# Copies ahead of exponentials, attention's first steps before the loop's turn, and scans and outer products spread singly over the steps

## The chip, the core and the metric

The kernel runs on one core of a Trainium2 chip. The core has engines that work side by side and meet only at semaphores: TensorE (PE, matrix products and transposes, results in PSUM), VectorE (DVE), ScalarE (ACT, exponentials and copies), GpSimd (POOL) and SyncE (SP, which issues most DMAs). Each engine works through its own instructions in program order. The metric is the device time of one launch in microseconds, the median of several runs; a profiled execution has a time of its own, and all rows below come from it.

## What is computed

Two layers run over 8 sequences of 512 tokens with 256 features. The change touches the second layer alone, and in it two parts that the kernel runs side by side for each sequence: a recurrence with a state of 16 by 16 for each of 16 heads, and causal softmax attention with 16 heads.

```python
# recurrence (the "scan"), for each head
def step(st, inp):
    rt, wt, kt, vt = inp
    kv = jnp.einsum('bhi,bhj->bhij', kt, vt)            # outer product
    y = jnp.einsum('bhi,bhij->bhj', rt, st + uh[None, :, :, None] * kv)
    return (wt[..., None] * st + kv, y)
...
# attention
q = jnp.concatenate([q_nope, _rope(q_rope)], axis=-1)
k = jnp.concatenate([kv, _rope(k_rope)], axis=-1)
att = jnp.einsum('bhqd,bhkd->bhqk', q, k) / jnp.sqrt(jnp.float32(D))
att = jnp.where(mask, att, jnp.float32(-jnp.inf))
att = jax.nn.softmax(att, axis=-1)
y = jnp.einsum('bhqk,bhkd->bhqd', att, v)
...
# what is around them
x = x + s * g        # s: recurrence, g: silu of (attention + experts)
```

## The kernel before

`phase_c` does the second layer, one sequence of 512 tokens after the other. For each engine it has two functions: `before_attention(b)` (projections, mixing, and the rotation of the queries) and `attention(b)` (attention, the recurrence, then gating and nine experts). Every engine calls `before_attention(0)`, then loops over `attention(b)` and `before_attention(b + 1)` for b = 0 to 6, and then calls `attention(7)`. So the turn of the loop, a branch on each engine, lies between `before_attention` and `attention`. The experts' part of `attention` is left as it is.

**Queries.** In `before_attention` PE makes eight products q0 to q7 (two heads each). DVE rotates them (`rotate`, L1700 and L1701: one product with the cosines, one shuffle), POOL finishes each (L1884, L1886). DVE's rotation n waits until POOL has finished rotation n-2, since there are two shuffle buffers. Between q5 and q6 DVE also does `outer(0)`, `scan(0)` and `outer(1)` of the recurrence.

**The 32 steps of attention.** A step i is a pair of heads and one tile of 128 queries; i % 4 sets how many keys it sees: 128, 256, 384 or 512. For one step:

- PE `scores(i)` (L1155, with the mask L1158): two score tiles in banks 0 and 1 for even i, 2 and 3 for odd i. It waits until `exp(i-2)` has read these banks.
- DVE `highest(i)` (L1631): the row maxima, read from PSUM.
- ACT `exp(i)` (L1454): two exponentials, into four probability tiles; it waits until those of step i-2 are transposed.
- PE `turn_probs(i)` (L1172): transposes the probabilities into banks 5 and 6. It waits for `exp(i)` and until the copies of step i-1 have freed the banks, and stands in PE's order right after `scores(i+2)`.
- ACT `keep(i)` (L1463): two copies of the transposed tiles to SBUF. They stand in ACT's order in front of `exp(i+3)`.

After every eight steps PE does `weigh_values(g)` (L1202, probabilities times values, 64 short products), which needs the copies of the group's last step; ACT copies its result (L1472), PE spreads the inverse row sums (`spread_inverse`, L1191), DVE scales (L1665). `weigh_values(0)` stands on PE behind `turn_probs(8)`, thus between `scores(10)` and `scores(11)`, and likewise 8 and 16 steps later.

**The recurrence beside it.** 32 units n, 24 of them during attention. One unit is DVE `outer(n)` (L1644, reads a copy of a value row that SP fetched, writes `kv`), DVE `scan(n)` (L1651, the recurrence over 512 tokens) and POOL `product(n)` (L1897, state times receptance); PE sums four products at a time (`reduce_state`, L1182). In three of four steps (`UNIT_STEP`, i % 4 not 3) DVE does `scan(n)` and `outer(n+1)` right after `highest(i)`; in the fourth it does `highest(i)` alone. `outer` and `scan` read two operands from SBUF, `highest` and the rotations read PSUM.

## Time and profile before

| | us |
|---|---|
| median of three runs | 2815.42 |
| lowest and highest run | 2812.85, 2822.94 |
| profiled execution | 2818.96 |
| its span in the trace | 2817.1 |
| PE busy in the span | 2302.9 (82%) |
| DVE busy | 1749.2 (62%) |
| ACT busy | 930.0 (33%) |
| POOL busy | 931.9 (33%) |

The span is what the trace covers; the 1.9 us beside it are outside the engines' work. A sequence of the second layer takes some 258 us, of which the 32 steps of attention take 96. The first exponential of the eight sequences starts at 805.00, 1066.66, 1324.93, 1581.95, 1840.59, 2099.63, 2359.03 and 2616.34 us.

### The profile page before, as it was taken

The numbers are of one execution on the slowest core, as the hardware profiler recorded it, in microseconds if no ns is written. First come the engines' busy times: TensorE is split into PE (matmuls) and PEld (weight loads), VectorE is DVE, ScalarE is ACT, GpSimd is POOL, SyncE is SP. The second block draws the span as 40 slices with busy tenths as digits, with TensorE's granted clock in tenths as the row PEclk, the third lists the DMA queues.
The fourth block names the chain that finished last, engine by engine and source line by source line (L and its number), as shares of the span: only waits on it lengthen the run. The fifth ranks groups of instructions, "written<-read, shape, count | busy, mean of one in ns | idle before, by whom it ended". The sixth has DMA issues, their size and how long they took to land.

```text
span 2817.1 us, 35706 instructions
## 1 busy us (share of the span) xinstructions
PE 2302.9 (82%) x9632; PEld 1248.1 (44%) x9633; DVE 1749.2 (62%) x2951; ACT 930.0 (33%) x2466; POOL 931.9 (33%) x722
## 2 busy tenths in 40 slices
PE   7887599996877886798889778967988897788777
PEld 3443366664434533443444345334434443453344
DVE  5777344443276657675756677576757566765766
ACT  2333133231135224412532351254125323522441
POOL 2113200001164245415432542453154325423531
PEclk9998799998788998898989899988989898999889
DMA  4342411013022112201210221122012102211210
GB/s 138 112 143 62 148 30 30 26 30 98 8 57 54 34 31 61 68 1 50 63 48 15 58 54 34 31 61 68 0 49 62 49 7 62 57 34 30 61 46 8
DMA packets 139997, 146.16 MB, mean 52 GB/s; under 512 B 47025, under 2 KB 99889, under 8 KB 139825
## 3 DMA queue, kind: packets, MB, share of 16 engines
q1 hardware_dynamic: 132530, 131.49, 17.2%
q0 software_dynamic: 3072, 8.41, 0.9%
q10 hardware_dynamic: 4224, 4.19, 0.4%
q8 instruction: 81, 1.33, 0.2%
q14 instruction: 90, 0.74, 0.1%
HBM read 116.48 MB, written 27.43 MB: 51 GB/s over the span
## 4 chain that ended last, share of the span: by engine, by line
PE 27%; issue 24%; DVE 10%; POOL 9%; ACT 4%; DVEq 0%; DMA 0%; POOLq 0%; ACTq 0%
PE bank L1284 13%; PE bank L1172 4%; DVE arena L1631 3%; POOL arena L1879 3%; PE bank L1155 3%; ACT arena L1454 3%; POOL arena L1884 2%; DVE arena L1651 2%; PE bank L1202 2%; DVE arena L1644 2%; PE bank L1182 2%; POOL arena L1886 2%; ACT arena L1463 1%; PE bank L1109 1%; PE bank L1191 1%
## 5 line engine op out<-in xcount | busy, mean ns | idle before, releaser
L1897 POOL TENSOR_TENSOR arena<-arena 128x512 f32<-128x512 f32 x256 | 385.1, 1505 | 619.5 <-DVE arena L1651 603.7
L1109 PE MATMUL bank<-arena 128*128 128x512 f32 (+2 forms) x896 | 444.5, 644 | 40.9 <-ACT arena L1415 22.2
L1284 PE MATMUL bank<-arena 128*128 128x512 f32 (+2 forms) x1312 | 445.6, 495 | 6.3 <-ACT arena L1419 6.3
L1454 ACT ACTIVATE arena<-bank,arena 128x128 f32<-128x128 f32 (+3 forms) x512 | 266.0, 524 | 468.3 <-DVE arena L1631 410.4
L1172 PE MATMUL bank<-arena 128*128 128x128 f32 x1280 | 234.8, 318 | 187.2 <-ACT arena L1463 185.9
L1651 DVE TENSOR_TENSOR_SCAN arena<-arena 128x512 f32<-128x512 f32 x256 | 346.4, 1353 | 8.1 <-issue 7.8
L1284 PEld LDWEIGHTS bank<-arena 128*128 128x128 f32 x1312 | 255.8, 209 | 190.9 <-issue 154.2
L1631 DVE TENSOR_REDUCE arena<-bank 128x2 f32<-128x256 f32 (+3 forms) x256 | 207.5, 821 | 190.4 <-PE bank L1158 177.3
L1109 PEld LDWEIGHTS bank<-arena 128*128 128x128 f32 (+2 forms) x896 | 166.3, 195 | 299.9 <-issue 235.4
L1155 PE MATMUL bank<-arena 64*128 64x128 f32 (+3 forms) x1024 | 235.1, 540 | 63.6 <-ACT arena L1454 63.6
L1172 PEld LDWEIGHTS bank<-arena 128*128 128x128 f32 x1280 | 168.9, 163 | 224.6 <-ACT arena L1454 190.3
L269 PE MATMUL bank<-arena 128*128 128x512 f32 x384 | 189.6, 647 | 34.3 <-DVE arena L423 18.0
L1644 DVE TENSOR_TENSOR arena<-arena 128x512 f32<-128x512 f32 x256 | 210.7, 823 | 0.0
L1463 ACT ACTIVATE arena<-bank 128x128 f32<-128x128 f32 (+3 forms) x512 | 197.1, 440 | 12.8 <-PE bank L1172 12.2
L1879 POOL TENSOR_TENSOR arena<-arena 128x512 f32<-128x512 f32 x80 | 103.2, 1309 | 220.2 <-DVE arena L1676 220.2
L1155 PEld LDWEIGHTS bank<-arena 64*128 64x128 f32 x1024 | 86.9, 208 | 145.1 <-ACT arena L1454 81.0
L702 PE MATMUL bank<-arena 128*128 x624 | 145.6, 385 | 1.3 <-ACT arena L736 1.3
L682 PE MATMUL bank<-arena 128*128 x312 | 143.5, 603 | 1.2 <-DVE arena L777 1.2
L1884 POOL TENSOR_TENSOR arena<-arena 128x512 f32<-128x512 f32 x72 | 103.6, 1438 | 116.4 <-DVE arena L1701 116.2
L1676 DVE SCALAR_TENSOR_TENSOR arena<-bank,arena 128x512 f32<-128x512 f32 x80 | 58.5, 741 | 128.8 <-PE bank L1109 126.1
L269 PEld LDWEIGHTS bank<-arena 128*128 128x128 f32 x384 | 75.9, 204 | 131.1 <-issue 90.4
L1415 ACT ACTIVATE arena<-bank 128x512 f32<-128x512 f32 (+1 forms) x96 | 55.6, 595 | 230.1 <-PE bank L1109 230.0
(201 smaller groups left out, 2955.8 us busy)
## 6 DMA issues: line engine op xcount, KB each, us to landing
arena<-values SPq DMA_DIRECT2D x256, 256.0 KB, 3.5
arena<-in_L_attn_h SPq DMA_DIRECT2D x16, 512.0 KB, 3.6
arena<-in_W1T SPq DMA_DIRECT2D x8, 1024.0 KB, 5.7
arena<-in_W2T SPq DMA_DIRECT2D x8, 1024.0 KB, 8.6
sorted_rows<-arena SPq DMA_DIRECT2D x42, 128.5 KB, 9.3
arena<-sorted_rows SPq DMA_DIRECT2D x40, 128.5 KB, 2.1
gate_rows<-arena SPq DMA_DIRECT2D x39, 128.0 KB, 1.7
s_rows<-arena ACTq DMA_DIRECT2D x8, 512.0 KB, 3.0
```

Of the source, the lines that this page charges most:

```text
L269: last = nc.tensor.matmul(bank[s + q][:, :], gru_w[layer][:, k, q * D + m * P:q * D + (m + 1) * P], src[:, k, :], start=(k == 0), stop=(k ...
L1109: last = nc.tensor.matmul(dst[rows, :], w, x, start=(n == 0), stop=(n == len(pairs) - 1))
L1155: nc.tensor.matmul(bank[2 * (i % LAG) + half][:, 0:n], qT[rows, p, qt * P:(qt + 1) * P], ckvT[rows, 0:n], start=True, stop=False)
L1172: last = nc.tensor.transpose(bank[5 + half][:, kt * P:(kt + 1) * P], probs[s % PROBS][:, kt * P:(kt + 1) * P], ident)
L1284: last = nc.tensor.matmul(dst[o], w, x, start=first, stop=last_one)
L1454: nc.scalar.activation(probs[s % PROBS][:, 0:n], bank[2 * (i % LAG) + half][:, 0:n], ACT.Exp, bias=neg_max[:, s:s + 1], accum_out=row_sum[ ...
L1463: nc.scalar.activation(turned[h % HGROUP][:, 0:qt + 1, qt * P:(qt + 1) * P], bank[5 + half][:, 0:(qt + 1) * P].rearrange("p (k c) -> p k c ...
L1631: nc.vector.tensor_reduce(neg_max[:, 2 * i:2 * i + 2], psum[:, at:at + 1024].rearrange("p (h k) -> p h k", h=2)[:, :, 0:n], X, ALU.max, ne ...
L1644: nc.vector.tensor_tensor(kv[n % 2], copies[n % COPIES], proj["k"][:, n // HD, :], ALU.mult).then_inc(kv_done, 1)
L1651: nc.vector.tensor_tensor_scan(state[n % STATES][:, 1:T + 1], proj["w"][:, m, :], kv[n % 2], VEC["init"][:, m * HD + j:m * HD + j + 1], AL ...
L1879: nc.gpsimd.tensor_tensor(mix[n % 2][:, m, :], mix[n % 2][:, m, :], xnT[:, m, :], ALU.add).then_inc(mixed, 1)
L1897: nc.gpsimd.tensor_tensor(prods[n % PRODS], state[n % STATES][:, 0:T], proj["r"][:, m, :], ALU.mult).then_inc(prod_done, 1)
```

## The change

Four edits, all in `phase_c`:

1. ACT does the copies `keep(i-2)` in front of `exp(i)`; before, it did `keep(i-3)` there.
2. PE issues `scores(0)` behind q5 and `scores(1)` behind q6, DVE does `highest(0)` behind the rotation of q5 and `highest(1)` behind that of q6, all of this before the turn of the loop. `outer(0)` moves to behind the rotation of q3; `scan(0)` and `outer(1)` move behind the turn, into step 1. DVE's wait on `w_step` goes to the end of `before_attention`.
3. `PARTS` spreads the outer products and scans: two of them in even steps and in steps 1 and 3, one in the other odd steps, in the order scan, outer, scan, outer. It is 24 scans and 24 outer products either way.
4. `weigh_values(g)` for g = 0, 1, 2 moves on PE from behind `turn_probs` to in front of `scores` of the same step (10, 18, 26). The last one stays behind the first part of the output product.

```diff
-UNIT_STEP = [i for i in range(PSTEPS) if i % NT != NT - 1]
-EARLY = len(UNIT_STEP)
+EARLY = 24
+def parts_by_step():
+    parts = [("scan", 0)]
+    for n in range(1, EARLY):
+        parts += [("outer", n), ("scan", n)]
+    parts.append(("outer", EARLY))
+    steps, at = [[]], 0
+    for i in range(1, PSTEPS):
+        n = 2 if i % 2 == 0 or i in (1, 3) else 1
+        steps.append(parts[at:at + n])
+        at += n
+    return steps
+PARTS = parts_by_step()
+UNIT_STEP = [i for i in range(PSTEPS) for name, n in PARTS[i] if name == "scan"]
...
@@ PE, before_attention
                         product(b, name, [(q_w[:, k, i * P:(i + 1) * P], xbT[:, k, :]) for k in range(KD)])
+                        if name in ("q5", "q6"):
+                            scores(b, int(name[1]) - 5)
@@ PE, attention
-                for i in range(PSTEPS + LAG + 3):
+                for i in range(LAG, PSTEPS + LAG + 3):
+                    if GSTEPS + 2 <= i < PSTEPS and (i - GSTEPS - 2) % GSTEPS == 0:
+                        weigh_values(b, (i - GSTEPS - 2) // GSTEPS)
                     if i < PSTEPS:
                         scores(b, i)
-                    if LAG <= i < PSTEPS + LAG:
+                    if i < PSTEPS + LAG:
                         turn_probs(b, i - LAG)
...
                         wo(1, 0, range(GROUPS - 1))
-                    if i >= GSTEPS + 2 and (i - GSTEPS - 2) % GSTEPS == 0:
-                        weigh_values(b, (i - GSTEPS - 2) // GSTEPS)
+                        weigh_values(b, GROUPS - 1)
@@ ACT, attention
-                    if LAG < i <= PSTEPS + LAG:
-                        keep(2 * (i - LAG - 1))
-                        keep(2 * (i - LAG - 1) + 1)
+                    if LAG <= i < PSTEPS + LAG:
+                        keep(2 * (i - LAG))
+                        keep(2 * (i - LAG) + 1)
                     if i < PSTEPS:
                         exp(2 * i)
                         exp(2 * i + 1)
@@ DVE, before_attention
-                        if name == "q5":
+                        if name == "q3":
                             outer(b, 0)
-                            v.wait_ge(w_step, 2 * b + 2)
-                            scan(b, 0)
-                            outer(b, 1)
+                        elif name in ("q5", "q6"):
+                            highest(b, m - 5)
+                v.wait_ge(w_step, 2 * b + 2)
@@ DVE, attention
-                    if i < PSTEPS:
+                    if LAG <= i < PSTEPS:
                         highest(b, i)
...
-                    if i in UNIT_STEP and i > 0:
-                        unit(b, UNIT_STEP.index(i))
+                    for name, n in PARTS[i] if i < PSTEPS else []:
+                        (scan if name == "scan" else outer)(b, n)
@@ POOL, attention
-                    if i in UNIT_STEP:
-                        product(UNIT_STEP.index(i))
+                    for n in [n for n in range(EARLY) if UNIT_STEP[n] == i]:
+                        product(n)
```

DVE around the turn of the loop, from the rotation of q4 on, before (L1700 and L1701 are a rotation, L1644 is `outer`, L1651 `scan`, L1631 `highest`; ISA and register rows are waits and branches):

```order
L1700 TENSOR_TENSOR arena<-bank,arena 128x512
L1701 STREAM_SHUFFLE arena<-bank 128x512
L1644 TENSOR_TENSOR arena<-arena 128x512
L1651 SCALAR_TENSOR_TENSOR arena<-arena 128x512
L1644 TENSOR_TENSOR arena<-arena 128x512
L1700 TENSOR_TENSOR arena<-bank,arena 128x512
L1701 STREAM_SHUFFLE arena<-bank 128x512
L1700 TENSOR_TENSOR arena<-bank,arena 128x512
L1701 STREAM_SHUFFLE arena<-bank 128x512
L1843 UNCONDITIONAL_BRANCH
L1843 ISA
L1631 TENSOR_REDUCE arena<-bank 128x2
```

and in the changed kernel, from the rotation of q5 on (lines are 21 higher: L1652 is `highest`, L1672 `scan`, L1665 `outer`, L1721 and L1722 a rotation):

```order
L1721 TENSOR_TENSOR arena<-bank,arena 128x512
L1722 STREAM_SHUFFLE arena<-bank 128x512
L1652 TENSOR_REDUCE arena<-bank 128x2
L1721 TENSOR_TENSOR arena<-bank,arena 128x512
L1722 STREAM_SHUFFLE arena<-bank 128x512
L1652 TENSOR_REDUCE arena<-bank 128x2
L1721 TENSOR_TENSOR arena<-bank,arena 128x512
L1722 STREAM_SHUFFLE arena<-bank 128x512
L1864 UNCONDITIONAL_BRANCH
L1864 ISA
L1672 SCALAR_TENSOR_TENSOR arena<-arena 128x512
```

Between the rotations of q5 and q6 three operations of the recurrence are gone and the first two maxima stand among the rotations instead; the first operation behind the branch is now a scan.

ACT's first steps of a sequence, before (L1454 are the exponentials, L1463 the copies; 128x2x128 is a copy of 256 columns):

```order
L1454 ACTIVATE arena<-bank,arena 128x128 x2
L1454 ACTIVATE arena<-bank,arena 128x256 x2
L1454 ACTIVATE arena<-bank,arena 128x384 x2
L1463 ACTIVATE arena<-bank 128x128 x2
L1454 ACTIVATE arena<-bank,arena 128x512 x2
L1463 ACTIVATE arena<-bank 128x2x128 x2
L1454 ACTIVATE arena<-bank,arena 128x128 x2
```

and in the changed kernel (L1475 exponentials, L1484 copies):

```order
L1475 ACTIVATE arena<-bank,arena 128x128 x2
L1475 ACTIVATE arena<-bank,arena 128x256 x2
L1484 ACTIVATE arena<-bank 128x128 x2
L1475 ACTIVATE arena<-bank,arena 128x384 x2
L1484 ACTIVATE arena<-bank 128x2x128 x2
L1475 ACTIVATE arena<-bank,arena 128x512 x2
L1484 ACTIVATE arena<-bank 128x3x128 x2
```

Each pair of copies now stands one pair of exponentials earlier.

PE at step 10, before (L1155 and L1158 are scores, L1172 transposes, L1202 `weigh_values`):

```order
L1155 MATMUL bank<-arena 128x384 x2
L1158 MATMUL bank<-arena 128x128 x2
L1168 REGISTER_ALU
L1172 MATMUL bank<-arena 128x128 x2
L1202 MATMUL bank<-arena 32x512 x4
```

and in the changed kernel (L1173 and L1176 scores, L1190 transposes, L1220 `weigh_values`):

```order
L1190 MATMUL bank<-arena 128x128 x8
L1220 MATMUL bank<-arena 32x512 x4
L1220 MATMUL bank<-arena 32x384 x4
L1220 MATMUL bank<-arena 32x256 x4
L1220 MATMUL bank<-arena 32x128 x4
L1170 REGISTER_ALU
L1173 MATMUL bank<-arena 128x384 x2
```

`weigh_values` now stands between the transposes of step 7 and the scores of step 10.

## Rows read from the trace of the kernel before

**Rows 1.** Busy us by stage: PE, weight loads, DVE, ACT, POOL; PEclk, DMA.

```profile
1066.60:1163.00 96.40, 72.16 (x486) 38.21 (x486) 73.64 (x88) 57.06 (x191) 44.05 (x30) 0.89 0.26 64
2099.17:2195.09 95.92, 73.48 (x486) 39.39 (x486) 72.16 (x86) 55.40 (x185) 43.98 (x29) 0.88 0.24 61
2108.00:2116.00 8.00, 5.90 (x26) 3.86 (x24) 4.84 (x7) 5.27 (x18) 2.30 (x3) 0.57 0.29 67
```

**Rows 2.** Waits from 2099 to 2197 us: who waited for whom, total, times, longest.

```profile
DVE arena L1631 <- PE bank L1158: 22.4, 15, 4.1
PE bank L1172 <- ACT arena L1463: 20.3, 24, 2.2
DVE arena L1651 <- issue: 1.3, 1, 1.3
```

**Rows 3.** Timeline (start, us, engine, line), exponentials of step 7 to those of step 9.

```profile
2120.44 0.69 ACT L1454 ACTIVATE arena<-bank,arena 128x512 f32<-128x512 f32 x1 [1.34 <-DVE arena L1631]
...
2121.72 1.27 DVE L1651 TENSOR_TENSOR_SCAN arena<-arena 128x512 f32<-128x512 f32 x1
2121.78 0.66 ACT L1463 ACTIVATE arena<-bank 128x256 f32<-128x256 f32 x2
2122.30 0.85 PE L1172 MATMUL bank<-arena 128*128 128x128 f32 x6 [0.96 <-ACT arena L1463]
...
2122.91 0.67 DVE L1644 TENSOR_TENSOR arena<-arena 128x512 f32<-128x512 f32 x1
2123.08 0.70 PE L1155 MATMUL bank<-arena 64*128 64x256 f32 x4
...
2124.04 0.69 DVE L1631 TENSOR_REDUCE arena<-bank 128x2 f32<-128x512 f32 x1 [0.46 <-PE bank L1158]
...
2124.86 0.47 ACT L1454 ACTIVATE arena<-bank,arena 128x256 f32<-128x256 f32 x1 [0.42 <-PE bank L1172]
```

**Rows 4.** Timeline around the turn of the loop.

```profile
2088.83 1.27 POOL L1884 TENSOR_TENSOR arena<-arena 128x512 f32<-128x512 f32 x1
...
2090.15 0.67 DVE L1644 TENSOR_TENSOR arena<-arena 128x512 f32<-128x512 f32 x1
...
2090.86 2.17 DVE L1651 TENSOR_TENSOR_SCAN arena<-arena 128x512 f32<-128x512 f32 x1
...
2096.41 0.74 DVE L1701 STREAM_SHUFFLE arena<-bank 128x512 f32<-128x512 f32 x1
...
2099.17 1.02 DVE L1631 TENSOR_REDUCE arena<-bank 128x2 f32<-128x256 f32 x2 [2.02 <-issue]
...
2101.52 2.23 DVE L1651 TENSOR_TENSOR_SCAN arena<-arena 128x512 f32<-128x512 f32 x1 [1.32 <-issue]
```

**Rows 5.** Timeline, the copies of step 7 and `weigh_values(0)` behind them.

```profile
2124.19 1.06 PE L1172 MATMUL bank<-arena 128*128 128x128 f32 x8 [0.19 <-ACT arena L1463]
...
2125.77 1.09 ACT L1463 ACTIVATE arena<-bank 128x512 f32<-128x512 f32 x2
...
2127.24 2.37 PE L1202 MATMUL bank<-arena 128*32 128x512 f32 x32
```

**Rows 6.** Chain that ended last (start, us, what): PE work between transposes and scores.

```profile
2134.97 0.89 PE bank L1191 x8
2135.86 1.00 PE bank L1182 x8
```

**Rows 7.** Timeline at the end of the steps.

```profile
2193.88 1.21 DVE L1631 TENSOR_REDUCE arena<-bank 128x2 f32<-128x1024 f32 x1
...
2196.37 1.63 POOL L1897 TENSOR_TENSOR arena<-arena 128x512 f32<-128x512 f32 x1 [1.45 <-DVE arena L1651]
...
2196.55 0.66 ACT L1463 ACTIVATE arena<-bank 128x256 f32<-128x256 f32 x2
...
2196.95 2.13 DVE L1651 TENSOR_TENSOR_SCAN arena<-arena 128x512 f32<-128x512 f32 x1
...
2198.27 1.94 PE L1172 MATMUL bank<-arena 128*128 128x128 f32 x8 [0.23 <-ACT arena L1463]
```

1 line of the change is left out of this document (added).

## The prediction, written before the changed kernel ran

> **What bounds the kernel now.** I read four views in this order: busy time by stage, the waits of the stage, the timeline of two steps, and the timeline around the turn of the loop. In the stage of the 32 steps, from the first `highest` at 2099.17 to the end of the last at 2195.09, no engine is full: of 95.92 us PE is busy 73.5, DVE 72.2, ACT 55.4, POOL 44.0, and another sequence shows the same [rows 1]. So the stage is bound by waiting in rings. DVE's idle time is 95.92 - 72.16 = 23.8 us; 22.4 of it is `highest` waiting for the scores, in 15 places, and 1.3 is a stall in which it waits for nothing shown [rows 2].
>
> Why the scores are late is seen in two steps [rows 3]. The exponentials of step 7 start at 2120.44. Behind them ACT does the copies of step 5 (2121.78), only then may PE transpose step 6 (2122.30, after 0.96 us of waiting for the copies), behind that stand the scores of step 9 (2123.08), then `highest(9)` (2124.04, 0.46 idle) and the exponentials of step 9 (2124.86). That ring takes 4.4 us for two steps, although the scores of step 9 need only the exponentials of step 7. PE waits 20.3 us in all for copies [rows 2].
>
> **Copies ahead of exponentials.** After the change the copies of step 5 stand in front of the exponentials of step 7, where ACT waits for `highest(7)` anyway. When the exponentials of step 7 end (2121.78), step 6 is no longer held up by a copy behind them. The ring that remains is exponentials, scores, then the later of two branches, exponentials. From the end of scores that see 256 keys, the longer branch is half the transposes of 512 columns (0.5), a hand-off (0.15) and both copies (1.09) [rows 5], then two exponentials of 256 (0.94), a hand-off and scores of 512 (about 1.3): 4.1 us. From there `highest` (1.21) [rows 7], exponentials of 512 (1.34, from 2120.44 to 2121.78), hand-offs and scores of 256 (0.85) [rows 3]: 3.7 us. Together 7.8 us for four steps, against 96/8 = 12.0 now. DVE's own work is 72.2/8 = 9.0 us for four steps. So DVE becomes the bound, with 1.2 us of slack for the ring.
>
> **Even spreading.** DVE's work is the same, but the port to SBUF that it shares with POOL now costs it something. In the trace a scan that started at 2196.95 inside a product of POOL's (2196.37 to 2198.00) took 2.13 us instead of 1.27, so that it ended 1.08 after the product did [rows 3, 7]. Before, `outer` follows its scan at once and is ahead of the product (1.27, then 0.67) [rows 3]. Singly spread, a product starts 0.15 us after its scan and runs 1.3 to 1.6 us, while DVE does only `highest` (0.4 to 1.2) before its next two-operand operation: that is caught for 0.2 to 0.5 us in three of four steps, 1.1 us per four steps. Where DVE has a wait or `scale_values` in between, it costs nothing; I take half, 0.5 us times 7 groups of four steps, 3.5 us (ends 0 and 7.7).
>
> The Trainium skill states this as a rule, in SBUF — State Buffer, section "Who interferes with whom": an exclusive lock of the shared port pair for a whole instruction when VectorE has two SBUF inputs and GpSimd reads SBUF. By that rule the change is charged in full, the 7.7 us end. The scan at 2196.95, which finished only after the product, agrees with it.
>
> **`weigh_values` in front of the scores.** This adds a wait, at steps 10, 18 and 26. From the end of `scores(9)` it takes the transposes' first half and the copies of step 7 (1.9, as above), a hand-off (0.1), 2.3 us of `weigh_values` (2127.24 to 2129.6) [rows 5], the scores of 384 keys (1.1) and a hand-off (0.1): 5.5 us until `highest(10)` may start. DVE has in this time, with 0.4 us of lag, `highest(9)` (0.61), a reciprocal (0.2) and a scan (1.2 to 1.5): 2.6 us. Behind the waiting `highest(10)` stand the outer product and scan of the step. DVE waits 2.8 us, three times: 8.4 (ends 5 and 10, by the lag). Other waits for scores: 0.6.
>
> **The beginning.** Before, DVE did outer, scan, outer from 2090.15 on, the scan at 2.17 instead of 1.27 since POOL was busy, and the rotation of q7 ended at 2097.15 [rows 4]. Now only the two `highest` (1.0 together) stand among the rotations, and POOL sets the pace: its first half for q4 starts at 2088.83, it takes 2 x 1.27 for each, so q5 is done at 2093.9. `outer(0)` behind q3 now runs beside POOL and puts it back by about 0.5: 2094.4. DVE's rotation of q7, 1.4 to 1.5, waits for that and ends at 2095.9, 1.25 us earlier. The turn's stall of 2.0 us [rows 4] stays; it comes in front of `scan(0)` now. The exponentials of steps 0 and 1 are done by then, but this brings nothing more: DVE is the bound here.
>
> **DVE's account of the stage.** From the end of the turn's stall to the end of the last `highest`: 72.2, less `highest` of steps 0 and 1 (1.0), plus `scan(0)` (1.2; `outer(1)` comes in, `outer(24)` goes out), plus the second stall (1.3), the port (3.5), and the waits (8.4 + 0.6): 86.2 us instead of 95.9. That is 9.7, with the beginning 1.2: 10.9 us.
>
> **The end.** After the exponentials of step 31, ACT still did the copies of step 29 (2196.55), PE transposed step 30, ACT copied it, and the transposes of step 31 started at 2198.27 [rows 7]. Now the copies of step 29 are done before. One copy and a hand-off plus half the transposes of step 30 go, about 1.0 us, and what follows (the rest of the sequence) is untouched and shifts as a whole. SP's fetches and POOL's products have time to spare: with four buffers of each, an operation of unit n waits for one of unit n-4, some 12 us back, and POOL is busy 44 of 96 us [rows 1].
>
> **Sum.** 10.9 + 1.0 = 11.9 us per sequence, times 8 = 95 us. Against the profiled 2818.96 this is 2724; it lies 3.5 us above the median 2815.42, so that the median should go to **2720** (-3.4%).
>
> **Rivals.**
>
> *PE's other work takes the place of the copies.* `reduce_state` (1.00, six times) and `spread_inverse` (0.89, three times) [rows 6] also stand between transposes and scores. The ring has only some 1.2 us of slack per four steps, and at steps 12 and 28 two of them come together. If all are exposed, 6.0 + 2.7 = 8.7 us of the gain go: 3.2 us per sequence, 26 us, 2790. For it: 0.89 and 1.00 stand on the chain that ended last in the trace of before. Against: that chain ran through them because the copies made PE late.
>
> *The port is paid in full.* 7.7 instead of 3.5, and `outer(0)` twice as dear: 7.2 us per sequence, 58 us, 2758. For it: the scan at 2196.95. Against: waits absorb part of it.
>
> *The change does little.* The exponentials wait for `turn_probs` of step i-2 as before, and now for the copies too. If hand-offs of the longer chain through both cost 0.3 us more in each of 32 steps (9.6), 2 us per sequence are left: 2800, within 0.5% or just beyond. Against: ACT is busy 55 of 96 us and has room [rows 1].
>
> *Slower: PE stays at its lower clock.* The granted clock is 0.88 in the stage and was 0.57 from 2108 to 2116 us [rows 1], after PE had waited for the first exponentials; 0.5 is the 1.2 GHz level, 1.0 is 2.4 GHz. PE's 73.5 busy us are 73.5 x 0.88 = 64.7 at full clock. If the new pattern of short pieces kept it at the lower level, PE would need 129 us: 33 more per sequence, 264 in all, 3080. It decides from a granted clock of 64.7/96 = 0.67 downward; at 0.60 it would be 12 us per sequence slower, 2910. Against: PE will wait less in total, not more.
>
> *More than forecast.* The port costs nothing (3.5 us), and the waits of `weigh_values` are at their lower end (3.4): some 16 us per sequence with a little for half-clock stretches that DVE now hides, 126 us, 2690.
>
> **Chances.** Forecast as worked out (9.5 to 14 us per sequence, 2704 to 2740) 0.48; port in full 0.20; PE's other work 0.13; little change 0.06; slower 0.05; more 0.08. The range goes from 2692 to 2788: it takes in the port in full and almost all of PE's other work. A measurement of this kernel can tell about 0.5% (14 us) from no change. Faster by more than that 0.88 (a third of "little change" and three quarters of PE's other work are in it), within it 0.07, slower 0.05.
>
> **What the profile after would show.** Right: DVE's wait for the scores falls from 22.4 to about 9 us per stage and stands at steps 10, 18 and 26, about 2.8 each; PE's wait for copies all but vanishes from the transposes; the stage takes 86 us; the rotation of q7 ends 1.2 us earlier against the rotation of q5. Port: means of L1672 and L1665 of some 1.4 and 0.8 us, with long ones inside products. PE's other work: `highest` waits at steps 8, 13, 18, 24 and 29 too. The prediction is wrong if the first steps after the turn stall for longer than 3.3 us, or if DVE waits for scores in most steps.

## The result, and the profile of the changed kernel

The changed kernel takes **2690.22 us** (median of four runs, 2685.88 to 2691.32) against 2814.14 (2808.63 to 2822.94) for the kernel before, measured side by side: the ratio is 0.9554, with a 95% interval of 0.9527 to 0.9581. That is 4.5% faster, where 3.4% and 2720 us were forecast. It lies 1.8 us below the low end of the range, 2692. The profiled execution took 2691.32 us, its span is 2689.5.

The eight first exponentials start at 787.67, 1032.59, 1274.48, 1517.99, 1762.48, 2006.04, 2250.72 and 2494.24 us. From the second to the seventh that is 243.6 us per sequence; before, it was (2359.03 - 1066.66)/5 = 258.5. So a sequence became 14.9 us shorter, not 11.9.

The stage first. This is the view of busy time by stretch that answers to [rows 1]: length, then busy us of PE, weight loads, DVE, ACT and POOL, then PEclk, DMA share and GB/s. The first row is the stage of the 32 steps in a typical sequence, from the first scan behind the turn to the end of the last `highest`; the other two are pieces of it around step 18.

```profile
1768.90:1852.00 83.10, 65.19 (x482) 35.66 (x480) 73.47 (x85) 53.14 (x178) 40.16 (x29) 0.92 0.27 74
1804.00:1810.00 6.00, 3.29 (x24) 1.94 (x26) 5.96 (x8) 3.70 (x13) 2.16 (x2) 1.00 0.19 48
1810.00:1813.60 3.60, 3.60 (x22) 1.67 (x26) 3.23 (x5) 3.35 (x12) 3.09 (x2) 0.65 0.52 146
```

DVE is now busy 73.5 of 83.1 us, 88%, where it was 75% of 95.9 [rows 1]. It is the bound, with 83.1 - 73.5 = 9.6 us of idle time. The waits of the stage (who waited for whom, total, times, longest; 1773.9 to 1852 us) say what that time is:

```profile
DVE arena L1652 <- PE bank L1176: 9.4, 4, 4.3
PE bank L1190 <- ACT arena L1484: 1.2, 1, 1.2
```

`highest` (L1652) waits 9.4 us for the scores (L1176), in four places, instead of 22.4 in 15 [rows 2]. The transposes (L1190) wait once for a copy (L1484), instead of 24 times for 20.3 us [rows 2]. The ring through the copies is gone. Three of the four waits in the timeline (start, us, engine, line, and in brackets the idle time before); the fourth is 0.32 us:

```profile
1794.71 0.96 DVE L1652 TENSOR_REDUCE arena<-bank 128x2 f32<-128x768 f32 x1 [2.69 <-PE bank L1176]
...
1817.52 0.96 DVE L1652 TENSOR_REDUCE arena<-bank 128x2 f32<-128x768 f32 x1 [4.30 <-PE bank L1176]
...
1838.37 0.96 DVE L1652 TENSOR_REDUCE arena<-bank 128x2 f32<-128x768 f32 x1 [2.05 <-PE bank L1176]
```

They are steps 10, 18 and 26, the steps in which `weigh_values` stands in front of the scores. The timeline of step 10 shows it, and answers to [rows 3, 5]:

```profile
1790.03 1.09 ACT L1484 ACTIVATE arena<-bank 128x512 f32<-128x512 f32 x2
...
1790.67 1.34 DVE L1672 TENSOR_TENSOR_SCAN arena<-arena 128x512 f32<-128x512 f32 x1
1790.90 1.97 POOL L1925 TENSOR_TENSOR arena<-arena 128x512 f32<-128x512 f32 x1
...
1791.24 2.36 PE L1220 MATMUL bank<-arena 128*32 128x512 f32 x32 [0.82 <-ACT arena L1484]
...
1793.54 0.92 PE L1173 MATMUL bank<-arena 64*128 64x384 f32 x4
```

The copies of step 7 end at 1791.12, `weigh_values(0)` (L1220) takes 2.36 us, and only then come the scores of step 10 (L1173, 1793.54), and `highest(10)` may start at 1794.71. DVE had finished its scan at 1792.01 and waited 2.7 us. (L1925 is POOL's widening of the inverse row sums; it matters below.)

Around the turn of the loop, the answer to [rows 4]:

```profile
1756.64 1.64 DVE L1665 TENSOR_TENSOR arena<-arena 128x512 f32<-128x512 f32 x1
...
1766.57 0.73 DVE L1722 STREAM_SHUFFLE arena<-bank 128x512 f32<-128x512 f32 x1
...
1768.92 1.89 DVE L1672 TENSOR_TENSOR_SCAN arena<-arena 128x512 f32<-128x512 f32 x1 [1.63 <-issue]
...
1770.73 1.68 DVE L1665 TENSOR_TENSOR arena<-arena 128x512 f32<-128x512 f32 x1
```

The rotation of q7 ends at 1767.30. Behind the branch DVE stalls for 1.63 us and then runs on without the second stall of 1.32 that [rows 4] shows.

At the end of the steps, the answer to [rows 7]:

```profile
1850.76 1.20 DVE L1652 TENSOR_REDUCE arena<-bank 128x2 f32<-128x1024 f32 x1
...
1853.97 1.94 PE L1190 MATMUL bank<-arena 128*128 128x128 f32 x8 [2.51 <-ACT arena L1484]
```

The last transposes start 1853.97 - 1851.96 = 2.0 us after the last `highest`; before it was 2198.27 - 2195.09 = 3.2 [rows 7].

### The profile page after: what moved, and what is told of

Same layout as the page of the kernel before. It is cut to its first block, busy times and chain, and to the rows that moved or that the text cites. A ratio compares the mean times of both kernels' runs of the same rounds, so it can differ in the third digit from the quotient of the medians.

```text
span 2689.5 us, 36104 instructions
## 1 busy us (share of the span) xinstructions
PE 2252.5 (84%) x9632; PEld 1219.3 (45%) x9633; DVE 1748.6 (65%) x2951; ACT 924.5 (34%) x2466; POOL 886.6 (33%) x722
## 3 DMA queue, kind: packets, MB, share of 16 engines
q8 instruction: 81, 1.33, 0.2%
## 4 chain that ended last, share of the span: by engine, by line
issue 26%; PE 24%; DVE 11%; POOL 10%; ACT 2%; DVEq 0%; DMA 0%; POOLq 0%; ACTq 0%
PE bank L1304 14%; DVE arena L1672 3%; DVE arena L1665 3%; POOL arena L1900 3%; POOL arena L1905 3%; DVE arena L1652 3%; PE bank L1220 2%; PE bank L1173 2%; POOL arena L1907 2%; PE bank L1127 1%; ACT arena L1475 1%; PE bank L1200 1%; PE bank L1190 1%; ACT arena L1484 1%; PE bank L1133 1%
## 5 line engine op out<-in xcount | busy, mean ns | idle before, releaser
L1918 POOL TENSOR_TENSOR arena<-arena 128x512 f32<-128x512 f32 x256 | 343.2, 1341 | 587.0 <-DVE arena L1672 574.8
L1672 DVE TENSOR_TENSOR_SCAN arena<-arena 128x512 f32<-128x512 f32 x256 | 356.4, 1392 | 12.2 <-issue 10.0
L1475 ACT ACTIVATE arena<-bank,arena 128x128 f32<-128x128 f32 (+3 forms) x512 | 266.3, 530 | 247.5 <-DVE arena L1652 247.5
L1304 PEld LDWEIGHTS bank<-arena 128*128 128x128 f32 x1312 | 256.4, 210 | 193.6 <-issue 157.1
L1173 PE MATMUL bank<-arena 64*128 64x128 f32 (+3 forms) x1024 | 223.7, 516 | 129.5 <-ACT arena L1475 119.8
L1652 DVE TENSOR_REDUCE arena<-bank 128x2 f32<-128x256 f32 (+3 forms) x256 | 207.5, 811 | 79.9 <-PE bank L1176 79.9
L1484 ACT ACTIVATE arena<-bank 128x128 f32<-128x128 f32 (+3 forms) x512 | 199.6, 442 | 121.0 <-PE bank L1190 120.9
L1190 PE MATMUL bank<-arena 128*128 128x128 f32 x1280 | 208.6, 300 | 36.9 <-ACT arena L1484 29.7
L1665 DVE TENSOR_TENSOR arena<-arena 128x512 f32<-128x512 f32 x256 | 204.2, 798 | 0.0
L1173 PEld LDWEIGHTS bank<-arena 64*128 64x128 f32 x1024 | 83.5, 199 | 220.4 <-ACT arena L1475 166.4
L1190 PEld LDWEIGHTS bank<-arena 128*128 128x128 f32 x1280 | 155.5, 155 | 45.0 <-ACT arena L1475 33.1
L1900 POOL TENSOR_TENSOR arena<-arena 128x512 f32<-128x512 f32 x80 | 103.1, 1309 | 214.2 <-DVE arena L1697 214.2
L1905 POOL TENSOR_TENSOR arena<-arena 128x512 f32<-128x512 f32 x72 | 99.9, 1388 | 113.2 <-DVE arena L1722 112.9
L269 PEld LDWEIGHTS bank<-arena 128*128 128x128 f32 x384 | 74.9, 201 | 127.5 <-issue 89.1
```

Of the source, the lines that this page charges most:

```text
L269: last = nc.tensor.matmul(bank[s + q][:, :], gru_w[layer][:, k, q * D + m * P:q * D + (m + 1) * P], src[:, k, :], start=(k == 0), stop=(k ...
L1173: nc.tensor.matmul(bank[2 * (i % LAG) + half][:, 0:n], qT[rows, p, qt * P:(qt + 1) * P], ckvT[rows, 0:n], start=True, stop=False)
L1190: last = nc.tensor.transpose(bank[5 + half][:, kt * P:(kt + 1) * P], probs[s % PROBS][:, kt * P:(kt + 1) * P], ident)
L1304: last = nc.tensor.matmul(dst[o], w, x, start=first, stop=last_one)
L1475: nc.scalar.activation(probs[s % PROBS][:, 0:n], bank[2 * (i % LAG) + half][:, 0:n], ACT.Exp, bias=neg_max[:, s:s + 1], accum_out=row_sum[ ...
L1484: nc.scalar.activation(turned[h % HGROUP][:, 0:qt + 1, qt * P:(qt + 1) * P], bank[5 + half][:, 0:(qt + 1) * P].rearrange("p (k c) -> p k c ...
```

## The account of one sequence

A mark that both kernels share is DVE's scaling of the transposed `xb` in `before_attention`: it stands behind the sequence's mixing and right ahead of the rotations. From it to the end of the last `highest` a typical sequence took 125.4 us before and takes 110.9 now, 14.5 less.

| part (us; stalls and ends: what is gained) | forecast | measured |
|---|---|---|
| rotation of q7 ends earlier | 1.25 | 1.28 |
| first stall behind the turn (2.0 before) shorter | 0 | 0.4 |
| second stall (1.3 before) gone | 0 | 1.3 |
| waits for the scores that remain (length) | 9.0 | 9.4 to 9.6 |
| stage from first scan to last `highest` (length) | 86.2 | 83.0 |
| mark to last `highest`, gain | 10.9 | 14.5 |
| end of the steps | 1.0 | -0.4 to 0.9 |
| whole sequence | 11.9 | 14.9 |

In the stage I had 77.2 us of DVE work with the port and the second stall in it; it is 73.5, 3.7 less: 1.3 of stall and 2.4 of port.

## Experiments

Every kernel ran beside the kernel before on one chip; the groups of experiments ran on different chips, whose medians for the kernel before lie between 2813.7 and 2816.1 us. The ratio to the kernel before is given with each. "Mark to last `highest`" is the length of the table above, for the typical sequences of the kernel's profile.

### How much the first phases scatter

Up to the first sequence of the second layer the two kernels run the same code, yet the first rotation of the changed kernel's profile came 9.8 us earlier (770.1 against 779.9). Is that the change or chance? The two kernels ran again, unchanged.

> The kernel before once more, unchanged, for a second profile. The profile after started the second layer's rotations 9.8 us earlier than the profile before (770.1 against 779.9 us), in phases that the change does not touch. Theory A (scatter from one execution to the next): this profile lies at 770 to 780 us for the first rotation. Theory B (the change moves code and so changes the first phases): it lies at 779 to 781 again.

> The changed kernel once more for a second profile: the first rotation lay at 770.1 us in the first one. Theory (scatter of the first phases): anywhere from 770 to 782 us, with the stage of 32 steps unchanged (110.9 us from the scaling of xb to the end of the last highest). Rival (the change moves code and so speeds the first phases): 769 to 771 again.

The kernel before took 2812.5 us, with its first rotation at 774.9 and 125.5 us from mark to last `highest`; the changed one took 2695.5, with the first rotation at 774.6 and 110.9. So the same program moves by 5 us, and over all fourteen profiles the first rotation lies between 770 and 782 us. It is chance: the length of a typical sequence repeats to 0.1 us, while the phases ahead of it scatter over 12 us, 0.4% of the whole. The 1.8 us by which the range was missed are less than that, and this second run lies inside it; the distance to the forecast of 2720 is not chance.

### The parts alone

**Copies ahead of exponentials alone**: the kernel before with this one edit.

```diff
-                    if LAG < i <= PSTEPS + LAG:
-                        keep(2 * (i - LAG - 1))
-                        keep(2 * (i - LAG - 1) + 1)
+                    if LAG <= i < PSTEPS + LAG:
+                        keep(2 * (i - LAG))
+                        keep(2 * (i - LAG) + 1)
```

> The kernel before with only the copies of step i-2 ahead of the exponentials of step i; weigh_values, first steps and recurrence stay as they were. Theory (the ring through the copies bound the stage): most of the gain, 8 to 10 of the 14.7 us per sequence, 2735 to 2750 us; waits of highest for scores fall from 22.4 to some 12 us. Rival (the gain lies at the turn of the loop): 2800 to 2815.

It took 2691.71 us (2688.81 to 2697.68), ratio 0.956 [0.9528, 0.9593]: the whole gain of the change, with one of its four edits. Mark to last `highest` is 110.4 us in the middle, 109.0 to 113.5 in the loop, although this kernel still has both stalls and the late rotation of q7. The waits of a stage (L1631 is `highest`, L1158 the scores, as in the kernel before) and the place where `weigh_values` (L1202) stands here, behind the scores of step 10 (L1155, 1796.98) and the transposes of step 8:

```profile
DVE arena L1631 <- PE bank L1158: 7.9, 9, 1.6
```

```profile
1796.98 0.92 PE L1155 MATMUL bank<-arena 64*128 64x384 f32 x4
...
1798.28 2.36 PE L1202 MATMUL bank<-arena 128*32 128x512 f32 x32
...
1799.49 0.95 DVE L1631 TENSOR_REDUCE arena<-bank 128x2 f32<-128x768 f32 x1
1800.36 1.27 DVE L1651 TENSOR_TENSOR_SCAN arena<-arena 128x512 f32<-128x512 f32 x1
```

`highest(10)` starts without a wait while PE is at `weigh_values`: that work lies wholly beside DVE's. My expectation was 43 to 58 us too slow, since I had credited the other edits with the rest.

**Even spreading alone**: `PARTS` in the kernel before, with `outer(0)`, `scan(0)` and `outer(1)` left ahead of the turn.

```diff
-UNIT_STEP = [i for i in range(PSTEPS) if i % NT != NT - 1]
+        n = 2 if i % 2 == 0 else 1
+        steps.append(parts[at:at + n])
...
-                    if i in UNIT_STEP and i > 0:
-                        unit(b, UNIT_STEP.index(i))
+                    for name, n in PARTS[i] if i < PSTEPS else []:
+                        (scan if name == "scan" else outer)(b, n)
```

> The kernel before with only the scans and outer products spread singly over the steps; copies behind the exponentials, as before. Theory: the ring through the copies is still there, so DVE's order moves nothing but its waits: 2800 to 2815. Rival (DVE's uneven order is what made scores late): 2760 to 2785.

2818.32 us over ten runs, ratio 1.0004 [0.9987, 1.0022]: no change. Its waits are those of [rows 2] (L1648 `highest`, L1175 scores, L1189 transposes, L1480 copies):

```profile
DVE arena L1648 <- PE bank L1175: 22.8, 13, 4.5
PE bank L1189 <- ACT arena L1480: 18.8, 24, 2.2
```

While DVE waits 22 us for scores, it doesn't matter in which steps its work stands.

**The first steps alone**: the second edit of the change in the kernel before, with scan and outer product in pairs in steps 1, 2, 3 and then three of four.

```diff
+    at = [1, 2, 3] + [i for i in range(4, PSTEPS) if i % NT != NT - 1]
+    for n, i in enumerate(at):
+        steps[i] = [("scan", n), ("outer", n + 1)]
...
-                        if name == "q5":
+                        if name == "q3":
                             outer(b, 0)
-                            v.wait_ge(w_step, 2 * b + 2)
-                            scan(b, 0)
-                            outer(b, 1)
+                        elif name in ("q5", "q6"):
+                            highest(b, m - 5)
```

> The kernel before with only the first steps moved ahead of the turn of the loop, scans and outer products in pairs as before. Theory: 1.3 us of the rotations, 0.4 and 1.3 us of the two stalls behind the turn, 3.0 us per sequence, 24 us: 2785 to 2795. Rival (the ring makes up for a late start): under 8 us, 2807 or more.

2793.69 us (2782.99 to 2798.36), ratio 0.9915 [0.9884, 0.9945]: 22 us, as expected. Mark to last `highest` is 122.1, 3.3 less than before. The row behind the turn (L1665 is the scan) shows one stall where there were two, and the waits show that the ring through the copies stands as it was (L1645 `highest`, L1184 transposes, L1477 copies):

```profile
1822.26 1.62 DVE L1665 TENSOR_TENSOR_SCAN arena<-arena 128x512 f32<-128x512 f32 x1 [1.88 <-issue]
```

```profile
PE bank L1184 <- ACT arena L1477: 23.5, 24, 5.8
DVE arena L1645 <- PE bank L1170: 20.1, 15, 4.1
```

So the sum of the parts, -124 for the copies, -22 for the first steps and 0 for spreading, is 22 us more than the change as a whole brought. If the parts simply added up, the fourth edit would cost that much. They don't quite, as the runs below show: the copies and the first steps together bring 131 us, not 146.

### What `weigh_values` in front of the scores costs

First on top of the copies alone, then taken out of the changed kernel in two ways.

```diff
                 for i in range(PSTEPS + LAG + 3):
+                    if GSTEPS + 2 <= i < PSTEPS and (i - GSTEPS - 2) % GSTEPS == 0:
+                        weigh_values(b, (i - GSTEPS - 2) // GSTEPS)
                     if i < PSTEPS:
```

> copies_only with weigh_values (0) to (2) in front of the scores of their step, and nothing else of the change. Theory (its place costs 5 to 6 us per sequence whatever the order of DVE): 2730 to 2742. Rival (it costs only when DVE is the bound everywhere, and copies_only has waits of its own, 7.9 us): 2700 to 2715.

2709.15 us (2706.08 to 2711.46), ratio 0.9616 [0.9598, 0.9634]: 17 us slower than the copies alone, in the range of the rival and not of the theory. The intervals are just apart. Mark to last `highest` goes to 113 to 114 us, the waits for scores from 7.9 to some 11.

The changed kernel with `weigh_values` 0 to 2 back behind the transposes, where they stood before:

```diff
-                    if GSTEPS + 2 <= i < PSTEPS and (i - GSTEPS - 2) % GSTEPS == 0:
-                        weigh_values(b, (i - GSTEPS - 2) // GSTEPS)
...
-                        weigh_values(b, GROUPS - 1)
+                    if i >= GSTEPS + 2 and (i - GSTEPS - 2) % GSTEPS == 0:
+                        weigh_values(b, (i - GSTEPS - 2) // GSTEPS)
```

> The changed kernel with weigh_values(0) to (2) behind turn_probs of their step, as in the kernel before. In the profile after, highest waits 9.4 us per sequence in the steps of weigh_values (2.7, 4.3, 2.05); in copies_only weigh_values ran behind scores and transposes while DVE had work. Theory (the position of weigh_values costs): these waits fall to under 4 us, 5 to 6 us per sequence, 2640 to 2655. Rival (PE must do it anyway, and the copies that wait for it then hold up the exponentials): 2685 to 2700.

2658.79 us (2651.40 to 2685.04), ratio 0.9475 [0.9416, 0.9535]: 31 us faster than the changed kernel, or 22 by the ratios. One of the four runs took 2685, so that the interval touches that of the changed kernel (from 0.9527); what decides is the profile, and the next run. Mark to last `highest` is, behind the first sequence, 104.6 in four and 106.1 to 107.7 in three, instead of 110.9 to 113.7. The row of the waits (here L1651 is `highest`):

```profile
DVE arena L1651 <- PE bank L1176: 2.2, 5, 0.7
```

9.4 us of waits became 2.2, and 110.9 became 104.6. The edit that was part of the change cost 6.3 us in a typical sequence, and it sits in the three waits that the prediction had priced at 8.4. I had counted them as the price of the new order without asking what the old place would cost once the copies were out of the way.

And between the scores and the transposes of the same step:

> The changed kernel with weigh_values between scores and turn_probs of steps 10, 18 and 26. highest of the step no longer waits for it, but the transposes, the copies behind them and the exponentials of the step do. Theory: DVE has 2.9 us of work per step pair before it needs the exponentials of step 10, so 3 to 5 us per sequence are won, 2650 to 2665. Rival (exponentials become late instead): within 8 us of 2690.

2655.05 us (2651.39 to 2666.69), ratio 0.943 [0.9403, 0.9456], 105.0 to 107.9 us per sequence: the same as behind the transposes, and here the interval is clear of the changed kernel's. What matters is that the scores stand ahead of `weigh_values`; whether the transposes do too can't be seen.

### What even spreading is worth when DVE is the bound

Spreading alone brought nothing since DVE waited. It might in the other kernels. First, pairs in the changed kernel, `weigh_values` still in front:

```diff
-    parts = [("scan", 0)]
-    for n in range(1, EARLY):
-        parts += [("outer", n), ("scan", n)]
...
+    at = [1, 2, 3] + [i for i in range(4, PSTEPS) if i % NT != NT - 1]
+    for n, i in enumerate(at):
+        steps[i] = [("scan", n), ("outer", n + 1)]
```

> The changed kernel with scans and outer products in pairs in three of four steps; weigh_values stays in front. In the profile after a scan took 1.40 us on average, in copies_only 1.35, since products of POOL run when the scan comes. Theory (the single spreading costs by the shared port, about 1.2 us per sequence): 2676 to 2684. Rival (it evens DVE's waits out and is worth something): 2695 to 2710.

2697.79 us (2687.53 to 2701.65), ratio 0.9574 [0.9542, 0.9605]. Neither theory's sign shows: mark to last `highest` is 111.0 in typical sequences, as in the changed kernel (110.9), and so are the waits (L1646 is `highest`):

```profile
DVE arena L1646 <- PE bank L1170: 9.4, 9, 3.4
```

The 7.6 us in the median are within what the first phases scatter; in this profile they ended 12 us later (first rotation at 782.4). In the stage the scan takes 1.33 us in the mean instead of 1.40 and `outer` 0.84 instead of 0.79; the two differences cancel.

What the two orders pay at the port is told under the port term below.

Then pairs with `weigh_values` behind, which is the copies and the first steps together:

> Copies ahead and the first steps ahead of the turn, but scans and outer products in pairs in three of four steps and weigh_values behind turn_probs, as in the kernel before. The two good parts together. Theory (weigh_values in front and the single spreading cost what the first steps gain): copies alone 2692 less 3.2 us per sequence, 2660 to 2672. Rival (the copies alone already use up what can be had, DVE's slack takes the start): 2685 to 2695.

2683.15 us (2675.97 to 2686.29), ratio 0.9538 [0.9512, 0.9564], longer than expected. The profile shows two lengths within one kernel, behind the first sequence: 106.05 us in three and 110.25 in four. This is the same stretch of a short sequence (first two rows) and of a long one (last two), the columns as above:

```profile
1794.25:1802.25 8.00, 4.91 (x38) 2.98 (x39) 7.61 (x11) 5.68 (x22) 4.09 (x3) 1.00 0.26 67
1802.25:1810.25 8.00, 7.86 (x73) 3.54 (x72) 7.42 (x10) 4.95 (x17) 5.32 (x4) 1.00 0.29 90
...
2032.70:2040.70 8.00, 4.92 (x32) 2.68 (x33) 7.24 (x10) 5.68 (x22) 4.09 (x3) 0.85 0.25 67
2040.70:2048.70 8.00, 8.00 (x60) 3.74 (x60) 6.09 (x7) 2.42 (x9) 4.39 (x4) 0.72 0.29 68
```

The granted clock stays at 1.00 in the one, and in the other it falls to 0.85 and 0.72 in the mean of a stretch: it is at its 1.2 GHz level (0.50) from 2038.29 to 2045.12. The pieces on PE's path show it, `reduce_state` (L1194) first in the short sequence, then in the long one:

```profile
1802.66 1.07 PE L1194 MATMUL bank<-arena 128*32 128x512 f32 x8
...
2042.56 1.94 PE L1194 MATMUL bank<-arena 128*32 128x512 f32 x8
```

DVE's busy time falls from 7.42 to 6.09 in that stretch, since it waits for scores. 4.2 us are lost in such a sequence. In the 8 us right ahead of the fall PE had been busy 6.00 us, and 5.99 in the same stretch of the short sequence. Why the clock fell in one and not in the other, no run here tells.

Against these, single spreading with `weigh_values` behind has 104.6 us (short) and 106.1 to 107.7 (long), and its long ones lie beside a fall too: 1.5 us better in the short ones, 2.5 to 4.1 in the long ones. Over the whole kernel it is 2683 to 2659, by intervals that overlap a little (0.9512 to 0.9564, 0.9416 to 0.9535), while the profiles show it in both kinds of sequence. So even spreading is worth something once nothing else holds DVE up. Whether it also softens a fall of the clock is not shown, since the falls were smaller there too: 0.92 in the mean of a long sequence's stage, against 0.89 with pairs (0.94 in the short ones of both). In the changed kernel the waits in front of `highest` in steps 10, 18 and 26 hide it.

### The port between DVE and POOL

I had charged the single order with 3.5 us of contention. How much of it is POOL's product? Here each product covers only 128 of its 512 columns; the other 384 are left out. The rest is the kernel with `weigh_values` behind.

```diff
-nc.gpsimd.tensor_tensor(prods[n % PRODS], state[n % STATES][:, 0:T], proj["r"][:, m, :], ALU.mult)
+nc.gpsimd.tensor_tensor(prods[n % PRODS][:, 0:P], state[n % STATES][:, 0:P], proj["r"][:, m, 0:P], ALU.mult)
```

> weigh_behind with POOL's products cut from 512 to 128 columns; the other 384 columns of each product are left out, so that the recurrence's output lacks them. It measures the price of the shared port under the products alone. In weigh_behind a scan takes 1.39 and an outer product 0.82 us on average against 1.27 and 0.67 undisturbed, 6.5 us per sequence, of which the rotations and three widenings of the inverse row sums make about 4. Theory (products that run under the single parts cost little, since a product alone takes 1.09 us): 0.5 to 2.5 us per sequence, 2638 to 2655. Rival (port paid as the prediction charged it, 3.5 us): under 2632.

2632.32 us (2629.75 to 2634.55), ratio 0.9346 [0.9328, 0.9364]: 26 us less. But the stage did not get shorter: mark to last `highest` is 104.1 to 107.2, against 104.6 to 107.7. The groups of all scans (busy us, mean ns), first with whole products, then with short ones:

```profile
L1671 DVE TENSOR_TENSOR_SCAN arena<-arena 128x512 f32<-128x512 f32 x256 | 355.0, 1387 | 12.3 <-issue 10.0
```

```profile
L1671 DVE TENSOR_TENSOR_SCAN arena<-arena 128x512 f32<-128x512 f32 x256 | 329.6, 1287 | 13.0 <-issue 10.7
```

The products cost a scan 0.1 us in the mean. Summed over a typical stage, the scans get 2.5 us shorter and the outer products 1.7, so that whole products cost DVE 4.2 us in this kernel, more than the theory's 0.5 to 2.5. But what DVE saves it waits for scores instead: its wait rises from 2.2 to 5.7 us. Of the 21 us between the two profiled executions (2653.91 and 2632.99), 6.6 are an earlier end of the first phases; the rest lies outside the steps of attention, and its place is open. The 2632.32 lies at the edge of the rival's range: DVE's operations got shorter by what the rival said and more, but attention did not.

What a product costs the next operation is seen in two places of the kernel with `weigh_values` behind (L1917 product, L1664 `outer`, L1671 scan, L1651 `highest`):

```profile
1821.53 1.20 DVE L1651 TENSOR_REDUCE arena<-bank 128x2 f32<-128x1024 f32 x1
1821.69 1.09 POOL L1917 TENSOR_TENSOR arena<-arena 128x512 f32<-128x512 f32 x1 [2.20 <-DVE arena L1671]
...
1822.64 0.69 DVE L1664 TENSOR_TENSOR arena<-arena 128x512 f32<-128x512 f32 x1
...
1824.57 0.67 DVE L1664 TENSOR_TENSOR arena<-arena 128x512 f32<-128x512 f32 x1
1824.73 1.63 POOL L1917 TENSOR_TENSOR arena<-arena 128x512 f32<-128x512 f32 x1 [1.95 <-DVE arena L1671]
...
1825.32 2.13 DVE L1671 TENSOR_TENSOR_SCAN arena<-arena 128x512 f32<-128x512 f32 x1
```

A product beside a `highest` takes 1.09 us, and the `outer` behind it still takes 0.69, its usual length. A product that starts 0.16 us into an `outer` takes 1.63: it ends at 1826.36, 1.12 after the `outer` ended at 1825.24. That fits a product that did nothing while the `outer` ran and then took its 1.09. The scan behind it in turn ends 1.09 after the product. The Trainium skill, in SBUF — State Buffer, "Who interferes with whom", says that the one which comes second is blocked until the first has finished its instruction; these rows agree with that, in both directions: a product behind an `outer`, and a scan behind a product.

### The last `weigh_values`

At the end of the steps the last `weigh_values` stands behind the first part of the output product. In the kernel with `weigh_values` behind, it is moved ahead of `mean0` (the mean of the recurrence's output), and that part of the output product behind the last `spread_inverse`:

```diff
                     if i == PSTEPS + LAG:
+                        weigh_values(b, GROUPS - 1)
                         pe.wait_ge(y_read, 2 * b + 1)
...
-                        wo(0, 0, range(GROUPS - 1))
-                        wo(1, 0, range(GROUPS - 1))
...
+                    if i == PSTEPS + LAG + 2:
+                        wo(0, 0, range(GROUPS - 1))
+                        wo(1, 0, range(GROUPS - 1))
```

> weigh_behind with the last weigh_values of a sequence in front of mean0, and the first part of the output product behind spread_inverse, where PE otherwise waits for ACT (0.8 us) and DVE (0.8 us). Theory: 1.2 to 1.6 us per sequence, 2645 to 2650. Rival (what follows is bound elsewhere, by mean0 and the recurrence): 2655 to 2662.

**2619.16 us** (2612.17 to 2629.12), ratio 0.9312 [0.9287, 0.9337]: the fastest kernel of the study, 6.9% below the kernel before and 2.5% below the changed one (0.9312 against 0.9554). First the place with `weigh_values` (L1220) late, at the end of one sequence of the kernel above (L1316 output product, L1209 `spread_inverse`, L1766 and L1767 the addition of its result):

```profile
1832.00 2.36 PE L1220 MATMUL bank<-arena 128*32 128x512 f32 x32
...
1835.17 1.13 PE L1209 MATMUL bank<-arena 128*128 128x128 f32 x8 [0.81 <-ACT arena L1492]
...
1837.08 3.29 PE L1316 MATMUL bank<-arena 128*128 128x256 f32 x14 [0.78 <-DVE arena L1685]
1839.55 0.69 DVE L1766 TENSOR_TENSOR arena<-arena,bank 128x512 f32<-128x512 f32 x1 [2.52 <-PE bank L1316]
```

and with it first:

```profile
2280.96 2.33 PE L1220 MATMUL bank<-arena 128*32 128x512 f32 x32
...
2285.07 7.07 PE L1316 MATMUL bank<-arena 128*128 128x256 f32 x32
...
2290.02 0.69 DVE L1767 TENSOR_TENSOR arena<-arena,bank 128x512 f32<-128x512 f32 x1 [4.06 <-PE bank L1316]
```

PE no longer waits 0.81 and 0.78 us for the chain through the copy and the scaling; the output product runs in one piece of 7.07 us. From the last `highest` to the addition of its result it is now 14.5 us instead of 16.8. That is 2.3 x 8 = 18 of the 40 us. The two profiles, 41.7 us apart, place the rest: a period from mark to mark is 233.5 instead of 237.8 in the mean of six, so 2 us more per sequence than tail and attention account for, and 9.5 us lie ahead of the second sequence's mark, 2.3 of them the first sequence's tail. The mean granted clock is 0.932 instead of 0.915. The clock is not the whole of it: the slowest run of this kernel had 0.918 and took 2629.12 us, the fastest of the kernel above had 0.915 and took 2651.40, and these 22 us are about the 18 of the tail. Whether PE's fewer gaps held the clock up in the other runs, or chance did, is not settled. The theory behind this run gave 12 us, and the mechanism it named brought 18.

## Why the prediction was right, and where it was not

**Right: the ring through the copies.** The prediction said that the copies stood in a ring of exponentials, copies, transposes and scores, that DVE would become the bound, and that the transposes would hardly wait for copies. The waits after show each point (20.3 us in 24 places to 1.2 in one; DVE 75% to 88% busy), and the copies alone give -124 us. That the copies alone would give all of it was not in the prediction.

**Right: the beginning.** The rotation of q7 ends 1.28 us earlier (forecast 1.25). `outer(0)` beside POOL takes 1.64 us, and delayed what follows by some 0.45 (forecast 0.5).

**Right in place and sum, wrong in evenness: the waits of `weigh_values`.** They stand at steps 10, 18 and 26, 9.0 us in all (2.69 + 4.30 + 2.05; forecast 8.4). Step 18 is dearer since the granted clock was 0.65 from 1810.0 to 1813.6, behind 6 us in which PE had been busy for 3.3. `reduce_state`, which stands there between the transposes and `weigh_values`, then took 1.94 us and not 1.0:

```profile
1811.94 1.94 PE L1200 MATMUL bank<-arena 128*32 128x512 f32 x8
```

That is the rival of PE's other work, in one place and in half. Elsewhere it doesn't show.

**Wrong: the term for the port.** This step failed first. The sum put 3.5 us on top of DVE's 72.4 us of operations (72.2 - 1.0 + 1.2); DVE was busy 73.5, so the whole term came to 1.1. It was not the products that cost less than thought. Scans beyond 1.27 us and outer products beyond 0.66 that met a product of POOL's add up to 3.3 us in the typical stage of the changed kernel (2.4 and 0.9), and the means of 1.40 and 0.79 us are the sign that the prediction gave for the port. What failed is that the term was added to a busy time which already held delays of the same kind, 3.5 us by the same count in the sequence of [rows 1]. The largest part of them were three outer products, each 1.47 us instead of 0.66, that POOL's widening of the inverse row sums held up (L1904 before, L1925 after); 2.4 us in all. One of the three, before:

```profile
2124.97 1.87 POOL L1904 TENSOR_TENSOR arena<-arena 128x512 f32<-128x512 f32 x1 [0.44 <-DVE arena L1637]
...
2125.92 1.47 DVE L1644 TENSOR_TENSOR arena<-arena 128x512 f32<-128x512 f32 x1
```

In pairs the outer product follows the scan at once and runs into the widening. In the single order `highest` follows: the widening at 1790.90 above ends at 1792.87, and the next `outer` starts at 1795.59. So these 2.4 us went, the products' share rose from 1.3 to 3.3, and 1.6 are new at the turn, where the first scan (1.89) and `outer` (1.68) meet the end of POOL's last rotation: 5.1 us against 3.5. (The 1.1 is a little less than this difference, since busy time counts overlapping instructions once.) The pairs in the changed kernel show the exchange with nothing else changed: 1.0 us by products and 2.4 by widenings, against 3.3 and none, and the sequence is as long. The length of a product in the term, "1.3 to 1.6 us", was also too long for over half of them: 14 of the 24 don't start inside an `outer` and take 1.09 to 1.28. 2.4 us per sequence too much are 19 us.

**Wrong: the second stall.** I took 1.3 us for a stall that comes anyway, after the first operations behind the turn. With the scan first behind the branch it is gone, and the first stall is 1.6 to 1.9 instead of 2.0 to 2.3; this holds in the changed kernel and with the first steps alone. Why is open. The loop's branch is taken six times (the first and the last sequence show no stall in either kernel), and 1.7 us at each are 10 us.

With these two terms put right a typical sequence comes out: 11.9 forecast, plus 2.4 and 1.7, less 0.6 for the waits and some 0.5 for the end, is 14.9. Eight of these are 119 us. The spans differ by 2817.1 - 2689.5 = 127.6, of which 9.8 are the scatter of the first phases; the first and the last sequence have no stall to lose, and gain less.

**Right at the same clock: the end.** The last transposes came 1.2 us earlier after the last `highest` (forecast 1.0). At the addition of the output product between 0.9 us of gain and 0.4 of loss are left, and the granted clock decides which: from the last `highest` to the end of that addition it takes 18.4 us before, with a granted clock of 0.90 in this stretch, 17.5 after where the clock is 0.90 too, and 18.1 to 18.7 after where it is 0.81.

**The rival that won** is the one called "more than forecast", 2690 us at a chance of 0.08, and that its number fits is luck. Its terms were the port at nothing and the waits of `weigh_values` 3.4 us lower; the port came to 1.1 and the waits were not lower but 0.6 higher, and the vanished stall took their place. Its sum is also wrong: 11.9 + 3.5 + 3.4 is 18.8 us per sequence and not 16, which gives 2665. And the range stopped at 2692, above this rival's own 2690. A stall and a port term each rounded toward cost stood in the sum, and a gain larger than the sum deserved more than 0.08. The full charge of 7.7 us, the other end of the port term, didn't come either: products held up 14 of the stage's operations, by 0.07 to 0.5 us, and not one in three of four steps.

**What the prediction didn't ask.** It priced all four edits as a whole, and so missed that one of them works against the others. The time of the change came out 30 us too long; the reasons were right for one edit. The copies alone give the gain, and `weigh_values` in front of the scores takes back, at 17 to 31 us, what the first steps and the spreading bring. The 8.4 us stood in my own sum as the largest loss. To set against it the price of leaving `weigh_values` where it was would have needed one line of the same working: behind the scores of step 10 it has 2.4 us in which DVE does `highest(10)` and a scan or an outer product (0.95 + 1.3), so it costs almost nothing.

## What to carry to other kernels

When a ring is opened, the work behind it changes its bound: price each further edit against the kernel in which the ring is already open, and also price leaving it out. A long piece of work that nobody waits for belongs behind the short piece that the bound engine waits for, as `weigh_values` behind the scores. And before a cost is added to a busy time, look what the busy time already holds of the same kind: the 72.2 us held 3.5 us of delays at the port, and the new order shed most of them while it took on others. The same goes for a single duration: a product of 1.6 us was one of 1.1 that had been blocked.

## What the runs showed of the hardware

- **DVE stalls behind a loop's taken branch, and a second time or not by what stands first.** With `highest` first, it stalled for 2.0 to 2.3 us and, two maxima later, for 1.2 to 1.5; with a scan first, for 1.6 to 1.9 once. This holds at six of six turns in each profile, and sequences without a taken branch ahead show neither. All were read from "issue" rows, where nothing shown is waited for; the cause is not shown.
- **Two operations with two SBUF operands, one on DVE and one on POOL, run one after the other.** Behind the end of the one before, a product takes its own 1.09 us, a scan about 1.1 and an outer product about 0.55.
- **The granted clock falls inside a stage in some sequences and not in others of the same kernel.** A sequence with a fall is 4.2 us longer where DVE's operations stand in pairs (0.89 in the stage instead of 0.94), and 1.5 to 3.1 where they are spread (0.92 instead of 0.94).
- **Identical first phases scatter by up to 12 us** between executions, while a sequence repeats to 0.1 us where the clock does. A difference under 0.5% is read from the periods of the profile rather than from the total.
